# A two-layer AdaLN transformer block pair on one core: 69 of the 175 products of a constant left out of the last attention phase

## The reference, cut to what matters

```
q, k, v, w = ...                                    # projections, normed; d = 8
A = solve_triangular(L, Rhs, lower=True, unit_diagonal=True)
qw = where(tri, einsum('bhid,bhtd->bhit', q, w), 0.0)
S = einsum('bhid,bhjd->bhij', q, k) - einsum('bhit,bhtj->bhij', qw, beta[..., None] * A)
G = cumsum(g, axis=-1)
logits = S * scale + (G[..., :, None] - G[..., None, :])
logits = where(tri, logits, -1e+30)
P = softmax(logits, axis=-1)
o = einsum('bhij,bhjd->bhid', P, v)
x = x + ga * (o.transpose(0, 2, 1, 3).reshape(B, T, D) @ Wo)
```

## Time and profile before

| | us |
|---|---|
| median of 3 runs | 2206.35 |
| lowest and highest | 2200.0, 2207.12 |
| the profiled execution, its own time | 2211.93 |
| its span | 2210.1 |
| last attention phase, TensorE's first product of the constant to the start of the experts | 1388.3 to 1560.3 |
| first to last group of maxima off the diagonal | 1436.7 to 1473.6 |

### The profile page before, as it was taken

The page is one execution under the profiler, slowest core; times in us unless marked ns, Lnnn a source line. Parts: engine busy times, 40 slices in busy tenths (PEclk is TensorE's granted clock), DMA queues, the critical chain, the costliest instruction groups (busy, mean ns, idle before and its releaser), DMA issues. The chain is left out here.

```text
span 2210.1 us, 43938 instructions
## 1 busy us (share of the span) xinstructions
PE 1998.4 (90%) x16519; PEld 1336.5 (60%) x16519; DVE 1590.3 (72%) x3657; ACT 860.3 (39%) x1686; POOL 763.0 (35%) x823
## 2 busy tenths in 40 slices
PE   4898998898898999899889889989899999699996
PEld 2573564565465456356456546765799999445543
DVE  6969759948948966975994894541366766799996
ACT  2022233224134133223323423313156665498893
POOL 2523512641551451353254155040256665100000
PEclk7998999999899889899999989988899999899998
DMA  3000000000000000000000000030622222301000
GB/s 115 11 1 16 1 2 16 4 20 16 1 21 12 6 21 2 15 9 15 16 3 20 16 1 22 8 136 1 241 69 72 72 71 64 97 20 44 5 11 19
DMA packets 70177, 72.46 MB, mean 33 GB/s; under 512 B 12976, under 2 KB 58592, under 8 KB 69840
## 3 DMA queue, kind: packets, MB, share of 16 engines
q1 hardware_dynamic: 61296, 51.75, 7.8%
q0 software_dynamic: 8672, 17.91, 2.3%
HBM read 38.05 MB, written 27.43 MB: 30 GB/s over the span
## 5 line engine op out<-in xcount | busy, mean ns | idle before, releaser
L669 ACT ACTIVATE a_prep<-ps 128x1536 f32<-128x1536 f32 (+1 forms) x112 | 155.5, 1389 | 329.8 <-PE ps L1304 216.0
L897 DVE TENSOR_REDUCE a_mpart<-ps 128x4 f32<-128x512 f32 (+1 forms) x320 | 190.6, 654 | 51.8 <-PE ps L1245 36.3
L1839 ACT ACTIVATE b_hid<-ps,b_stage 128x128 f32<-128x128 f32 x572 | 163.0, 367 | 138.9 <-PE ps L1954 138.9
L1824 POOL DMA_INDIRECT rows_y<-b_orow,b_target x143 | 164.0, 1147 | 119.1 <-DVE b_orow L1929 116.3
L482 POOL TENSOR_TENSOR a_X<-a_X,a_txy 128x480 f32<-128x480 f32 (+14 forms) x240 | 180.9, 771 | 60.2 <-DVE a_txy L847 58.8
L476 POOL TENSOR_TENSOR a_K<-a_K,a_yU 128x480 f32<-128x480 f32 (+14 forms) x120 | 83.6, 697 | 311.6 <-DVE a_yU L842 310.5
L1117 PE MATMUL ps<-a_txy,cst 128*128 128x480 f32 (+14 forms) x480 | 177.6, 476 | 11.1 <-DVE a_txy L829 10.4
L1954 PE MATMUL ps<-b_hTp,b_stage 128*128 128x128 f32 x1144 | 152.8, 277 | 0.0
L1963 PE MATMUL ps<-b_stage,b_hid 128*128 128x128 f32 x1144 | 151.4, 275 | 0.3 <-ACT b_hid L1839 0.3
L864 DVE TENSOR_TENSOR a_mats<-ps,cst 128x512 f32<-128x512 f32 x112 | 69.9, 683 | 112.4 <-PE ps L1146 112.4
L1954 PEld LDWEIGHTS ps<-b_hTp,b_stage 128*128 128x128 f32 x1144 | 140.7, 194 | 0.0
(11 more groups left out here) (462 smaller groups left out, 4359.2 us busy)
## 6 DMA issues: line engine op xcount, KB each, us to landing
b_hrow<-rows_h SPq DMA_DIRECT2D x143, 65.0 KB, 1.8
b_w<-in_wexp SPq DMA_DIRECT2D x16, 514.0 KB, 10.1
d_got<-rows_y SPq DMA_DIRECT2D x32, 256.0 KB, 3.8
rows_h<-a_txy SPq DMA_DIRECT2D x19, 325.0 KB, 2.9
rows_y<-b_orow,b_target POOLq DMA_INDIRECT x143, 2.4
out<-xs SPq DMA_DIRECT2D x8, 256.0 KB, 2.3
cst<-in_const SPq DMA_DIRECT2D x1, 1865.5 KB, 14.5
rows_h<-a_mats,r_slot POOLq DMA_INDIRECT x112
```

What stands on the lines that cost most here:

```text
L669: nc.scalar.activation(Pt[:, at:at + width, :], ps[:, 4:4 + width, :], ACT.Exp).then_inc(e_exp.sem, width)
L897: nc.vector.tensor_reduce(mpart[:, i, j, 4 * g:4 * g + 4], ps[:, 4 + n % 4, :].rearrange("p (r j) -> p r j", r=4)[:, :, 0:128 if i != j el ...
L1824: nc.gpsimd.indirect_dma_start(yrows, bass.IndirectOffsetOnAxis(target[:, p % DEEP:p % DEEP + 1], 0), orow[:, p % DEEP, :], None).then_inc ...
L1839: last = nc.scalar.activation(hid[:, p % 2, f, :], ps[:, p % 2, 128 * f:128 * f + 128], ACT.Gelu, bias=stage[:, p % 3, AT_B1 + f:AT_B1 + f ...
```

## The change

The string of TensorE for the last phase loses 69 letters `w`, and nothing else changes: 49 between the first group of maxima off the diagonal and L1258, and 20 of the 23 between L1258 and L1264. The other 106 products of the constant stay.

```
 ORDER_END = {
     'pe': ('bwwwwbbbbbbbbbbbbwbbbbbbbbwbbbbbbbbbbbbbwwwbbwwwwbbbbbbwwbwwbwwbwbbrwwwbwwbwwbrwwbrbwwwwwwbwwbwwbwwb'
-           'brwwwbbwwbrwbbrbbbbbwwbwwbwwbwwbbwbwwbwwbwwwwbbwbwwbwwwwwwbwbbwwwwwwwwwwwwwwbwwwwwbbwwbbwwwwwwwwwwww'
+           'brwwwbbwwbrbbrbbbbbbbbbbbbbbbbbbbbbbbbbwwwbbwwwwwbbbbbbbbbwwbbwbbwbwbbbbbbbbbwwwwwbbbbbbbwwbbbbwwwbb'
...
```

More of the change, by code:

```diff
@@ L184 @@
     'pe': ('bwwwwbbbbbbbbbbbbwbbbbbbbbwbbbbbbbbbbbbbwwwbbwwwwbbbbbbwwbwwbwwbwbbrwwwbwwbwwbrwwbrbwwwwwwbwwbwwbwwb'
-           'brwwwbbwwbrwbbrbbbbbwwbwwbwwbwwbbwbwwbwwbwwwwbbwbwwbwwwwwwbwbbwwwwwwwwwwwwwwbwwwwwbbwwbbwwwwwwwwwwww'
-           'wwwwwwwwwwwbbwwwwwbbbbbbbbbwwbbwbbwbwbbbbbbbbbwwwwwbbbbbbbwwbbbbwwwbbbbbbbbbbwwwwbbbbbbwbbbbbbbbwbbb'
-           'bbbbwwbbbbbbbwwbbbbbbbwwwwbbbbbbbbbwbbbbbwwwbbbbbbbwwbbbbbbbbbbbbwwwbbbbbwwwwwwwwwwbwwwwb'),
+           'brwwwbbwwbrbbrbbbbbbbbbbbbbbbbbbbbbbbbbwwwbbwwwwwbbbbbbbbbwwbbwbbwbwbbbbbbbbbwwwwwbbbbbbbwwbbbbwwwbb'
+           'bbbbbbbbwwwwbbbbbbwbbbbbbbbwbbbbbbbwwbbbbbbbwwbbbbbbbwwwwbbbbbbbbbwbbbbbwwwbbbbbbbwwbbbbbbbbbbbbwwwb'
+           'bbbbwwwwwwwwwwbwwwwb'),
     've': ('bbbbbbbbbbbbbrbrbbrbbbbbbrbrbrrrrrrrrrbrbrbrrbrrrrbrbrbrbrrrbbbbbbbbbbbbbbbbbbbbbbbbbbbbbbbbbbbbbbbb'
```

## The result

| | before | changed |
|---|---|---|
| median of 20 runs each, us | 2207.77 | 2196.09 |
| lowest and highest | 2200.0, 2215.6 | 2187.77, 2208.87 |
| profiled execution, its own time | 2211.93 | 2192.08 |
| its span | 2210.1 | 2190.3 |

The ratio is 0.9948, with a 95% interval of 0.9934 to 0.9962: 11.5 us faster, 8 to 15 by the interval.

A forecast was written before the change was run, and what follows sets the result against it. The constant's products on TensorE were taken to delay VectorE's maxima; GpSimd, next late, caps the gain at 12.5 us (10.5 from the maxima plus 1.97 of waiting), with 0 behind: 2206.35 - 12.5 = 2193.9 us, range 2187 to 2202.

The forecast's parts named there:

- Term 1: Off-diagonal maxima, second to sixth group: 29.44 us becomes 18.9 at the low clock, saving 10.5 (14.3 at the high clock).
- Term 2: Last maxima to transposes: L1264 starts about 0.1 us after the subtraction, 5.1 us gained; with the maxima 15.6 us early.
- Term 3: L1264 to L1279 at the low clock: 2.3 us lost, so L1279 is 13.3 us early on TensorE's path.
- Term 4: GpSimd's adds from L502: at most 12.5 us early (10.5 plus 1.97 of waiting), which decides the second pass's start.
- Behind it: From the second pass (L1295) on: nothing changes, counted as 0 with 3 us either side; its start moves by 12.5 us.
- The rival with the low clock behind the maxima: Low clock lasts into the spread products or second pass: gain 4 to 10 us, time 2198 to 2202; chance 0.21.
- No gain: Between and behind the maxima, left-out products only filled TensorE's waits: time within 6 us of 2206; chance 0.09.
- Slower: Clock stays at 0.50 through the second pass, each further low-clock us costing 0.7; in full 2245 us; chance 0.05.

The follow-up runs named there:

- the block: Changed kernel with 14 products of the constant in one block between second and third group of maxima; last group 0.3 us later, no whole-kernel time given.
- the pairs: Changed kernel with each L1245 issued directly behind the L1240 of its own bank, for the off-diagonal groups of the last phase; ratio 0.9925 to the first kernel.
- the one without the 46: Changed kernel also without the 46 products of the constant from the phase's start to the first off-diagonal group; ratio 0.9962 to the first kernel.
- the one with both edits: Changed kernel with each L1245 directly behind its L1240 and six GpSimd transfers put behind all its adds; ratio 0.9905 to the first kernel.

## Why the prediction was right

**Time.** Forecast 2193.9 (2187 to 2202) from a gain of 12.5 us; measured 2196.09 and 11.5 us. Of the 2.2 us between the times 1.4 are the first kernel's median, 2206.35 over 3 runs and 2207.77 over 20; the rest is the smaller gain, 11.7 us between the medians.

**Term 1, right.** From the second to the sixth group 18.6 us (1456.39 - 1437.79), forecast 18.9 at the low clock, before 29.4. The choice of the low clock is shown by the 27.2 us at 0.50, and by the block, which raised it for one period only.

**Term 2, right.** L1264 right behind L917. L1258 took 0.69 us, and L917 came 0.26 us later for it (forecast 0.2).

**Term 3, off in size.** L1264 to L1279 took 3.5 us, forecast 4.5. I had the clock rise as L1279 starts; it rose at 1464.1, 1.1 us ahead of L1279, and 1.1 us at the high clock do what takes 2.1 at the low one. The three products ahead of L1264 had started at 1460.14, 4.0 us before that rise; in the first kernel the products started at 1474.67, 3.9 us before the rise at 1478.6. I had taken from that stretch only its 3.3 us at 0.50. On TensorE's path L1279 is therefore 14.6 us early and not 13.3, which gained nothing, since this path was not the later one. The Trainium skill says in "TensorE: Matmul & The Clock Gate" ("Part 4: PE-mode transpose") that transposes don't count as busy in the same way. No delay from that shows here: of the 4.0 us 1.8 were the transposes of L1264, and the rise came practically as soon as behind the products alone (3.9 us).

**Term 4, right.** L502 is 48.9 - 36.2 = 12.7 us early, forecast 12.5, with no wait left; the kernel with only the 20 left out shows the same cap by itself (5.1 us on TensorE, 1.9 us at L1295), and moving the transfers away lifts it.

**Behind it, off by 1.3 us.** L1295 is 11.4 us early and not 12.5. L502 to L1295 took 11.2 us, before 9.9: a low stretch (1474.4 to 1477.7) fell into the spread products, where I had counted on the high clock; with the pairs, where none fell there, it took 9.9 us again. All three profiles of the changed kernel have it there, and so has the one without the 46; it is 3.4 us long and comes some 42 us behind the first maximum. The rival with the low clock behind the maxima was right to that extent.

**The profile's own difference** was 2211.93 - 2192.08 = 19.9 us, well above the 11.7 of the medians. 11.4 are the change, 4.0 lie ahead of the stretch and 5.3 in the second pass, in unchanged code, and 0.9 are lost again behind. Whoever compares only these two profiles would take 20 us for the effect.

**The rivals.** "No gain" fell: the waits ended by L1245 shrank to 2.17 us. "Slower" fell, as far as these 69 go. Its mechanism is real: with none of the 106 the second pass took 9 to 14 us more, at a mean clock of 0.63. But its price was too high: I had 0.7 us for each further us at the low clock, and the profiles show 0.4.

## What to carry to other kernels

A product that only keeps the clock up is free where its engine waits, and delays its engine by its own length where the next instruction is ready; the idle time of the partner engine, and who ends it, tells which. How much of that delay reaches the end is set by the next wait: 5.1 us on TensorE were 1.9 at the second pass. Ask per stretch whether the products really bought the high clock: here they didn't for 17 us of fully busy TensorE, while the 106 others, at the head of the phase and behind its maxima, were worth 12 us together. And when a step on one engine comes earlier, look for the other queue that feeds the same consumer (here transfers on GpSimd), since it caps the gain.

## What the runs showed that I had not expected

- TensorE at 0.50 was busy for 17.00 of 17.00 us and stayed low, with products of 24 and of 32 rows among full ones, and so did the second profile of the first kernel (17 us); with 14 full products in one block the clock rose 2.4 us into the block. What made the difference is not shown.
- Four products of 32 rows each, issued one by one as their inputs came, overlapped as those issued together did: a pitch of 3.09 us for a group at the low clock.
- Where the clock falls repeats between executions up to a point. The first fall came 3.9 to 4.7 us behind the first off-diagonal maximum in all profiles of kernels with the products ahead of it, but for the one with both edits (1.8 us), while in the second pass the low time was 0 us twice and 14 us once for the same kernel.
